# Class attention with swapped context matmuls and spread denominators, and a projection stage with two sets of accumulators

## What is computed

```python
# token attention
scores = einsum('bqhd,bkhd->bhqk', q, k) / sqrt(d)
ctx = einsum('bhqk,bkhd->bqhd', softmax(scores), v)
y = ctx @ Wo.T + bo + emb
h = (y - y.mean((1, 2))) / sqrt(y.var((1, 2)) + 1e-5)     # over a whole sequence
# recurrent attention, its inputs, from x = layernorm(h) over the last axis
q, k = l2norm(x @ Wq), l2norm(x @ Wk)                     # per head
v = x @ Wv;  beta = sigmoid(x @ Wbeta);  gate = silu(x @ Wg)
```

## Time and profile before

| | us |
|---|---|
| median of three executions | 996.98 |
| profiled execution, its own time | 998.3 |
| its span in the profile | 996.3 |
| attention block, from 31.2 to 132.4 | 101.2 |
| statistics block, to 142.6 | 10.2 |
| projection block, to 268.1 | 125.5 |
| PE, DVE, ACT, POOL busy over the span | 761.4, 669.1, 309.6, 424.3 |

### The profile page before, as it was taken

One profiled execution on the slowest core, in us unless ns is written; L12 is line 12 of the kernel. 1 busy time (PEld: TensorE's weight loads), 2 busy tenths in 40 slices (PEclk: granted clock), 3 DMA queues, 4 the chain that ended last, 5 costly groups with the idle time before them and its releaser, 6 DMA issues. The chain is left out here.

```text
span 996.3 us, 20604 instructions
## 1 busy us (share of the span) xinstructions
PE 761.4 (76%) x7708; PEld 521.3 (52%) x7708; DVE 669.1 (67%) x1047; ACT 309.6 (31%) x488; POOL 424.3 (43%) x225
## 2 busy tenths in 40 slices
PE   3589856677588888888888888885777659968653
PEld 3478733333366666666666666664555433322221
DVE  2697756767789999999999999992556530100104
ACT  2433403323233333333333333332444421110100
POOL 1543100000069999999999999982111100000000
PEclk9686978888899999999999999995999978976875
DMA  4000010000000100000000000002911059999946
GB/s 98 1 0 0 0 43 0 0 0 0 13 7 12 34 13 11 11 11 11 11 11 11 11 11 11 12 12 66 359 32 44 1 192 386 410 414 420 409 172 211
DMA packets 48889, 86.31 MB, mean 87 GB/s; under 512 B 5232, under 2 KB 32432, under 8 KB 48848
## 3 DMA queue, kind: packets, MB, share of 16 engines
q1 hardware_dynamic: 43248, 81.23, 22.1%
q10 hardware_dynamic: 5600, 4.53, 1.4%
HBM read 76.31 MB, written 9.44 MB: 86 GB/s over the span
## 5 line engine op out<-in xcount | busy, mean ns | idle before, releaser
L809 POOL TENSOR_TENSOR read<-state,q_pos 128x1024 f32<-128x1024 f32 x128 | 301.7, 2361 | 43.6 <-DVE state L904 34.5
L904 DVE TENSOR_TENSOR_SCAN state<-fac,ps_up 128x1024 f32<-128x1024 f32 x128 | 291.7, 2282 | 12.3 <-ACT fac L853 8.4
L853 ACT ACTIVATE fac<-ps_xf 128x1016 f32<-128x1016 f32 x128 | 130.3, 1018 | 232.1 <-PE ps_xf L934 232.1
L934 PE MATMUL ps_up<-hot,utab 64*128 64x128 f32 x2048 | 148.4, 284 | 38.0 <-DVE state L904 35.6
L934 PEld LDWEIGHTS ps_up<-hot,utab 64*128 64x128 f32 x2048 | 126.6, 189 | 88.6 <-DVE state L904 49.5
L934 PE MATMUL ps_xf<-hot,xtab 64*128 64x128 f32 x2048 | 139.1, 275 | 0.0
L818 POOL TENSOR_TENSOR utab<-tab 128x1024 f32 (+1 forms) x32 | 64.5, 2015 | 160.0 <-SPq L85 160.0
L934 PEld LDWEIGHTS ps_xf<-hot,xtab 64*128 64x128 f32 x2048 | 127.1, 189 | 0.8
L975 PE MATMUL ps_o<-read,sel 128*32 128x256 f32 x1024 | 81.8, 392 | 4.2 <-POOL read L809 4.2
L895 DVE TENSOR_TENSOR xtab<-tab,ps_k 128x1024 f32<-128x1024 f32 x64 | 76.6, 1197 | 1.5 <-PE ps_k L926 1.5
L373 POOL TENSOR_TENSOR logit<-score,logc 128x1024 f32<-128x1024 f32 x16 | 39.4, 2470 | 63.5 <-ACT prob L433 38.1
(11 more groups left out here) (206 smaller groups left out, 969.7 us busy)
## 6 DMA issues: line engine op xcount, KB each, us to landing
w_sb<-in_L_ffn_w SPq DMA_DIRECT2D x32, 2048.0 KB, 19.4
rec_out<-osb SPq DMA_DIRECT2D x128, 32.0 KB, 1.5
ao<-rec_out SPq DMA_DIRECT2D x8, 512.0 KB, 4.0
out_dram<-res ACTq DMA_DIRECT2D x8, 512.0 KB, 2.8
tok<-in_x SPq DMA_DIRECT2D x2, 512.0 KB, 8.3
exp_out<-eo SPq DMA_DIRECT2D x8, 128.0 KB
oq<-exp_out SPq DMA_DIRECT2D x2, 512.0 KB, 3.7
w_nat<-in_L_tok_Wq SPq DMA_DIRECT2D x1, 256.0 KB, 9.7
```

Of the source, the lines that this page charges most:

```text
L809: nc.gpsimd.tensor_tensor(read[n % 2][:], state[n % 4][:].rearrange("p (b i t) -> p b i t", b=2, i=IB), q_pos[x.s][:, :, x.k].unsqueeze(2) ...
L853: nc.scalar.activation(fac[n % 2][:].rearrange("p (n t) -> p n t", t=T)[:, :, 1:], ps_x[:].rearrange("p (n t) -> p n t", t=T)[:, :, 1:], A ...
L904: nc.vector.tensor_tensor_scan(state[n % 4][:], fac[n % 2][:], ps_u[n % 2][:], 0.0, ALU.mult, ALU.add)\
L934: last = nc.tensor.matmul(dst[:, b * 512 + col * T:b * 512 + (col + 1) * T], stationary[rows], pos[rows], start=True, stop=True)
```

## The change

In attention:

- The context matmuls swap operands. The stationary operand is now `v_pair` of a head pair (32 columns), the moving one the transposed probability (128 columns), and the result lands in the 32 PSUM partitions of column group `q = g % 4`. The context comes out transposed, so the transposes (L488) and the copies (L444) go. A second set of eight matmuls with `ones_pair` gives the denominators, each repeated over the 16 rows of its head: 32 instructions a pair instead of 16, and a denominator tile of 256 columns.
- The reciprocal is therefore taken over 128x256 elements instead of 128x16.
- The maxima go to PSUM (`ps_top`), so that the subtraction has one input in SBUF and one in PSUM.
- `ps_t` exists once instead of twice. The copy of the row into `h_tab` moves from DVE to ACT (`keep_row`).
- All engines step by pair: DVE does softmax of a pair, `output` of the pair two before, `finish` of the pair before. The last softmax is followed by two half turns instead of two turns.

In the inputs of the recurrence:

- Statistics and loop are one block. The row's own inverse root is taken from the same call of `inverse_root` as the sequence's (32 elements), so one call and four operations go.
- `x1` is formed straight from the raw row; the normalised row in `h_tab` is written by ACT in the loop (`hidden_rows`).
- `ps_qk`, `ps_vg` and the beta accumulator exist twice. PE waits separately for the copy of q, k and for v, gate; ACT squares first and copies q, k straight into `tab`.
- The norms of both pairs of a turn are found in one pass (64 elements), and rows are normalised two turns ahead.
- The activation table is loaded once, before the loop.

```diff
-            nc.vector.tensor_tensor(v_pair[:, :, 0:2 * D].rearrange("p g (s d) -> p g s d", d=D),
-                                    v_tab[:].rearrange("p (g s d) -> p g s d", s=2, d=D),
+            nc.vector.tensor_tensor(v_pair[:], v_tab[:].rearrange("p (g s d) -> p g s d", s=2, d=D),
                                     half.unsqueeze(3).broadcast_to([P, HP, 2, D]), ALU.mult)
-            ch.link(nc.vector.tensor_copy(v_pair[:, :, 2 * D:], half.broadcast_to([P, HP, 2])))
+            ch.link(nc.vector.tensor_copy(ones_pair[:], row_half[:].unsqueeze(2).broadcast_to([P, 2, D])))
...
-        ps_t = [ctx.enter_context(nc.psum_tensor(f"ps_t{i}", [P, HP * P], F32)) for i in range(2)]
-        ps_c = [ctx.enter_context(nc.psum_tensor(f"ps_c{i}", [P, 512], F32)) for i in range(2)]
+        ps_t = ctx.enter_context(nc.psum_tensor("ps_t", [P, HP * P], F32))
+        ps_c = [ctx.enter_context(nc.psum_tensor(f"ps_c{i}", [P, 2, KT, P], F32)) for i in range(2)]
+        ps_top = ctx.enter_context(nc.psum_tensor("ps_top", [P, 512], F32))
...
+            with eng.Fori(1, TURNS) as t:
+                if enter:
+                    enter(t)
+                for s in range(2):
+                    work(t, s, True, True, True)
+            return [(TURNS, s, False, s == 0, True) for s in range(2)]
...
+                top = ps_top[:, s * H:(s + 1) * H]
                 dve.wait_ge(sc_ok[s], START + i + 1)
-                ch.link(nc.vector.reduce_max(top[s][:], logit[s][:], AX.X))
-                nc.vector.tensor_tensor(logit[s][:], logit[s][:], top[s][:].unsqueeze(2).broadcast_to([P, H, C]),
+                ch.link(nc.vector.reduce_max(top, logit[s][:], AX.X))
+                nc.vector.tensor_tensor(logit[s][:], logit[s][:], top.unsqueeze(2).broadcast_to([P, H, C]),
                                         ALU.subtract).then_inc(lg_ok[s], 1)
 
             def finish(i, s):
                 dve.wait_ge(cx_mm[s], START + i + 1)
-                c = ps_c[s][:, 0:HP * (2 * D + 2)].rearrange("p (g n) -> p g n", g=HP)
-                ch.link(nc.vector.reciprocal(rden[s][:], c[:, :, 2 * D:]))
-                nc.vector.tensor_tensor(cx[s][:].rearrange("p (g s d) -> p g s d", s=2, d=D),
-                                        c[:, :, 0:2 * D].rearrange("p g (s d) -> p g s d", d=D),
-                                        rden[s][:].unsqueeze(3).broadcast_to([P, HP, 2, D]),
-                                        ALU.mult).then_inc(cx_ok[s], 1)
-
-            def output(i, s, r):
+                ch.link(nc.vector.reciprocal(rden[s][:], ps_c[s][:, 1].rearrange("p k c -> p (k c)")))
+                nc.vector.tensor_tensor(cx_t[s][:].rearrange("p k c -> p (k c)"),
+                                        ps_c[s][:, 0].rearrange("p k c -> p (k c)"), rden[s][:], ALU.mult)\
+                    .then_inc(cx_ok[s], 1)
...
                 dve.wait_ge(y_mm[s], START + i + 1)
-                ch.link(nc.vector.tensor_tensor(yrow[s][:], ps_y[s][:, E:2 * E], base[:], ALU.add))
+                dve.wait_ge(h_ok[s], START + i)
+                nc.vector.tensor_tensor(yrow[s][:], ps_y[s][:, 0:E], base[:], ALU.add).then_inc(y_ok[s], 1)
+                dve.wait_ge(y_ok[s], START + i + 1)
                 ch.link(nc.vector.bn_stats(bn[s][:], yrow[s][:]))
-                nc.vector.tensor_copy(stats6[:, bass.ds(r, 1)], bn[s][:].unsqueeze(1))
-                nc.vector.tensor_copy(h_tab[:, bass.ds(r, 1)], yrow[s][:].unsqueeze(1)).then_inc(y_ok[s], 1)
+                nc.vector.tensor_copy(stats6[:, bass.ds(2 * i + s, 1)], bn[s][:].unsqueeze(1))
+            def work(t, s, new, old, older):
                 if new:
-                    softmax_input(t, 0)
+                    softmax_input(t, s)
                 if older:
-                    for s in range(2):
-                        finish(t - 2, s)
-                if new:
-                    softmax_input(t, 1)
-                if older:
-                    for s in range(2):
-                        output(t - 2, s, 2 * (t - 2) + s)
-
-            step(0, older=False)
-            step(1, older=False)
-            with nc.vector.Fori(2, TURNS) as t:
-                ch.enter(t, 2 * 4, 2)
-                step(t)
+                    output(t - 1, s)
+                if old:
+                    finish(t - 1 + s, 1 - s)
...
+            def keep_row(i, s):
+                act.wait_ge(y_ok[s], START + i + 1)
+                nc.scalar.copy(h_tab[:, bass.ds(2 * i + s, 1)], yrow[s][:].unsqueeze(1)).then_inc(h_ok[s], 1)
+
+            def work(t, s, new, old, older):
                 if old:
-                    copy_prob(t - 1, 0)
+                    copy_prob(t - 1 + s, 1 - s)
                 if new:
-                    exponential(t, 0)
-                if old:
-                    copy_prob(t - 1, 1)
+                    exponential(t, s)
                 if older:
-                    for s in range(2):
-                        copy_context(t - 2, s)
...
         def _(pe):
             def transpose_prob(i, s):
                 pe.wait_ge(ex_ok[s], START + i + 1)
-                pe.wait_ge(pt_ok[s], START + i)
                 for g in range(HP):
-                    last = nc.tensor.transpose(ps_t[s][:, g * P:(g + 1) * P], prob[s][:, g * P:(g + 1) * P], ident[:])
+                    last = nc.tensor.transpose(ps_t[:, g * P:(g + 1) * P], prob[s][:, g * P:(g + 1) * P], ident[:])
                 last.then_inc(pt_mm[s], 1)
 
             def context(i, s):
                 pe.wait_ge(pt_ok[s], START + i + 1)
                 pe.wait_ge(cx_ok[s], START + i)
-                n = 2 * D + 2
-                for g in range(HP):
-                    last = nc.tensor.matmul(ps_c[s][:, g * n:(g + 1) * n], prob_t[s][:, g], v_pair[:, g],
-                                            start=True, stop=True)
+                for n in range(2):
+                    for g in range(HP):
+                        k, q = divmod(g, HP // KT)
+                        stationary = (ones_pair[:] if n else v_pair[:, g]).rearrange("p s d -> p (s d)")
+                        last = nc.tensor.matmul(ps_c[s][32 * q:32 * q + 32, n, k], stationary, prob_t[s][:, g],
+                                                start=True, stop=True)
...
+            def work(t, s, new, old, older):
+                if older:
+                    project(t - 1, s)
                 if old:
-                    for s in range(2):
-                        transpose_context(t - 1, s)
-                    for s in range(2):
-                        project(t - 1, s)
-
-            step(0, old=False)
-            with nc.tensor.Fori(1, TURNS) as t:
-                step(t)
-            step(TURNS, new=False)
+                    context(t - 1 + s, 1 - s)
+                if new:
+                    transpose_prob(t, s)
...
-            ch.link(nc.vector.tensor_scalar(varb[:], ps[:, 1, 0:PAIRS], EPS, None, ALU.add))
-            inverse_root(nc, ch, varb[:], rstd_b[:], ex2[:])
-
-            ch.link(nc.vector.tensor_tensor(mean_1[:], dm[:], rstd_b[:], ALU.mult))
-            ch.link(nc.vector.tensor_tensor(var1[:], var_r, rstd_b[:], ALU.mult))
-            ch.link(nc.vector.tensor_tensor(var1[:], var1[:], rstd_b[:], ALU.mult))
-            ch.link(nc.vector.tensor_scalar(var1[:], var1[:], EPS, None, ALU.add))
-            inverse_root(nc, ch, var1[:], rstd_1[:], ex2[:])
+            ch.link(nc.vector.tensor_scalar(varb[:, 0], ps[1][:, 0:PAIRS], EPS, None, ALU.add))
+
+            ch.link(nc.vector.scalar_tensor_tensor(varb[:, 1], varb[:, 0], EPS, var_r, ALU.mult, ALU.add))
+            flat = [v[:].rearrange("p n r -> p (n r)") for v in (varb, rstd)]
+            inverse_root(nc, ch, flat[0], flat[1], newton[:, 0:2 * PAIRS])
+            nc.vector.scalar_tensor_tensor(shift_b[:], mean_b[:], -1.0, rstd[:, 0], ALU.mult, ALU.mult)\
+                .then_inc(sh_ok, 1)
...
+                r = 2 * i + s
+                dve.wait_ge(xt_mm[s], START + i)
+                nc.vector.tensor_scalar(x1[s][:].unsqueeze(1), h_tab[:, bass.ds(r, 1)], mean_row[:, bass.ds(r, 1)],
+                                        rstd[:, 1, bass.ds(r, 1)], ALU.subtract, ALU.mult).then_inc(x_ok[s], 1)
...
+            def norms(i):
+
+                for s in range(2):
+                    dve.wait_ge(raw_ok[s], START + i + 1)
+                both = [v[:].rearrange("p s h -> p (s h)") for v in (norm2, rnorm)]
+                nc.vector.reduce_sum(both[0], sq[:].rearrange("p s h d -> p (s h) d"), AX.X).then_inc(rd_ok, 1)
+                dve.wait_ge(rd_ok, START + i + 1)
+                ch.link(nc.vector.tensor_scalar(both[0], both[0], 1e-24, None, ALU.max))
+                inverse_root(nc, ch, both[0], both[1], newton[:])
...
+                for s in range(2):
+                    values(i, s)
+                    if ahead:
+                        rows(i + 2, s)
+                norms(i)
+                for s in range(2):
+                    table(i, s)
...
```

(36 more changed lines are left out.)

256 lines of the change are left out of this document (101 added, 155 removed).

## The result

The changed kernel takes 963.38 us (median of 4 runs, 960.83 to 964.76), the kernel before 996.75 us in the runs beside it (4 runs, 993.08 to 998.99): a ratio of 0.966, 95% interval 0.963 to 0.969. The profiled execution took 960.83 us, 2.1 of it outside its span.

A forecast was written before the change was run, and what follows sets the result against it. Orders of waits were taken to bound both stages, with DVE working without a gap in attention. From 998.3 us, attention gives -1 and statistics with loop -31.8, making 965.5 us; range 950 to 981.

The forecast's parts named there:

- Reciprocal: Attention, on DVE: growing from 16 to 256 elements, it takes 1.64 us at 5.8 ns for each further element.
- Rivals A: Attention: the reciprocal is cheap (0.5 us), the PE chain bounds, 947 us in all; chance 0.08.
- B: Attention: the reciprocal's slope is steeper, 8.2 ns an element, 2.2 us for 256, 975 us in all; chance 0.10.
- Half turn of attention: Attention: DVE's softmax, `output` and `finish` sum to 5.58 us against 5.47 before, DVE still the bound.
- Subtraction: Attention: the other pair's subtraction loses its extra 1.08 us because one input moves to PSUM, as L895 shows.
- Rival D: Attention: the change does not remove the subtraction's port wait, PSUM operand or not; 974 to 983 us; chance 0.05.
- Rival C: Attention: small copy L413 meets POOL's L373 if `output` is 0.3 us late; in all half turns 995 us; chance 0.03.
- Statistics: Before the projection loop: fewer root operations and one barrier less save 3.9 us, first row for PE at 139.2.
- The weight loads: Statistics stage: issued at the start, they land in that time as before, so they cost nothing.
- What bounded the loop before: Projection loop, 15.25 us a turn: PE waits for single accumulators to be emptied, ACT pays a 1.28 us table load.
- The ring: Changed projection loop: the cycle of waits through ACT and DVE sets a turn of 11.1 us with semaphores.
- Rival E: Whole kernel slower: TensorE stays at 1.2 GHz and PE bounds the loop, 1013 us; chance 0.03.

The follow-up runs named there:

- recip_copy: Changed kernel with a copy of the same 256 denominators in place of their reciprocal (context scaled wrongly): 942.12 us.
- ctx_twice: Changed kernel with every context product of a pair issued twice, 64 matmuls instead of 32, same result: 965.46 us.
- Top_sbuf: Changed kernel with the maxima back in SBUF, in a tile of their own, instead of PSUM: 961.16 us.
- single_acc: Changed kernel with single instead of doubled accumulators for q, k and for v, g: 993.66 us.
- before_preload: Kernel before the change, with the Sigmoid table requested once ahead of its projection loop: 995.03 us.
- wait_hidden: Changed kernel with ScalarE's wait for tables moved from before the square to before the sigmoids, and both pairs' rows written after both activations: 952.19 us.

## Why the prediction was right, and where it was not

The time was forecast at 965.5 us and is 963.4; attention at -1 us (-0.3 in the profile; some +1 over the kernels of the table that leave its work alone), statistics and loop at -31.8 (-35.5). The total meets better than its terms, in part by luck: the forecast starts from the profiled execution, 998.3 us, 1.5 above the median; the two profiled executions differ by 37.5 us and the medians by 33.4, where 32.8 were forecast. So the terms count, not the 2 us. By the steps:

- **Reciprocal**: 1.64 us forecast from a slope of 5.8 ns, 1.75 measured at 6.25 ns. The two rows of other sizes gave the size of an instruction 16 times longer to 7%. Rivals A (0.5 us) and B (2.2 us) fall. VectorE: DVE Perf Modes of the Trainium skill (section "Walkthrough: the 8-slice pipeline in each mode") gives the division a repeat count of 8 and no time per element. The prediction's estimate of 2.13 us plus start-up takes that as 8 cycles an element, and is above what is measured: 6.25 ns are 6.0 cycles of the 0.96 GHz used there.
- **Half turn of attention**: 5.58 forecast, 5.65 measured; the excess is the reciprocal's. That VectorE stays the bound: shown (recip_copy, ctx_twice).
- **Subtraction "loses its extra 1.08 us because one input moves to PSUM"**: the size was right, the cause wrong. Top_sbuf has it without PSUM. The argument from L895 was sound about the hardware and did not ask whether the collision still occurs in the new order, which the same sum (addition from 3.75 us on, next subtraction at 5.6 + 1.2) would have told. Rival D, which priced PSUM as failing at 8 to 17 us, could for this reason not have come.
- **Rival C**, the small copy beside GpSimd: all 16 took 171 ns. The copy starts at 57.08, GpSimd at 57.39: the 0.3 us of the forecast, and no `output` was late enough to use them up.
- **Statistics**: 6.5 us forecast from first operation to first row, 136.55 - 130.13 = 6.4 measured (the forecast's own terms give 4.0 less, not 3.9). The weight loads, "I cost them at nothing": wrong, they became the wait.

```profile
138.21 1.12 PE L680 MATMUL ps_x<-ident,x 128*128 128x128 f32 x4 [4.68 <-DMA w_all<-in_L_attn_Wbeta]
```

  The row for TensorE is there at 136.55 + 0.41 = 136.96; its transposes wait until 138.21, 1.25 us longer, for the last weights. Two things meet. The statistics are shorter, 6.4 us instead of the 10.4 that covered the loads before. And the loads do not start "as before". The last of them, in the kernel before, then in the changed one:

```profile
134.78 0.47 SPq L553 DMA_DIRECT2D w_all<-in_L_attn_Wbeta  x1
```

```profile
133.96 0.47 SPq L548 DMA_DIRECT2D w_all<-in_L_attn_Wbeta  x1
```

  That is 2.1 us behind the first statistics operation (132.71) before, and 3.8 behind it (130.13) now; from issue to landing it takes 4.2 us in both. All eleven kernels here with the new stage issue the first load 1.9 us behind that operation, the three with the old one 0.1. Issued as before, the last weights would by these numbers (an estimate) have landed 6.3 us behind it, before the row was there at 6.8. Why the loads start later stays open. From the first row to the first values 10.25 us pass (136.55 to 146.80) where 7.4 stood (139.2 to 146.6); 1.25 is the weights, most of the rest the first projection, which takes 6.65 us (139.49 to 146.14), longer at the lower clock than in the kernel before, where it took 5.1 (144.91 to 150.00).
- **What bounded the loop before**: "PE waiting for ACT and DVE to empty the single accumulators" is borne out: in the old loop TensorE sat idle ahead of `ps_qk` for 6.5 us until VectorE's L629 and 5.7 us until ScalarE's L680, and in the new one single accumulators cost 29 us (single_acc). "ACT paying a table load of 1.28 us in each turn" is the step that failed. The load was seen on the engine and not asked whose work it delays (before_preload). The sum escaped the error because the new turn was built from its own ring, not by subtracting from the old one.
- **The ring**: 11.1 us forecast, 10.45 measured: the mis-sized term. ScalarE's part to the second pair's values is 1.61 + 2.07 = 3.7 us (168.11 to 169.72 to 171.79 in the same timeline) where 1.7 + 2.4 stood: the second pair's square starts 0.50 us after the rows begin, and operations of ScalarE overlap by up to 0.1 us each. VectorE's part is 178.56 - 171.79 = 6.77 against 6.85, and the 0.15 us added for semaphores did not come on top. From the second pair's first values to its last it is 72.0 us (150.90 to 222.91) where seven turns of 11.1 made 77.7: 5.7 less, of which the slower start of the loop takes back 2.6 and the end gives 0.6. That is the 3.7 us between 31.8 and 35.5.
- **"`hidden_rows` is on the ring, and if ACT were faster, DVE would be the bound at 9.4"**: wait_hidden shows VectorE as the bound, at 9.02, once the rows and the wait for the tables have moved; the share of the rows alone was not measured.
- **Rival E**, the lower clock: the loop had 0.88, and 1.00 in its middle turns. TensorE's pauses are shorter with two accumulators; with one, and the longer pauses, single_acc has 0.82. (The chances named for "faster" add up to 0.94 even without the half-effects, not to 0.93.)

Both errors of cause have one form: a long instruction was seen, and what it cost was taken from its length, not from what waited for its end.

## What to carry to other kernels

When a loop alternates between engines through one accumulator, doubling it can be worth more than thinning the work around it: here 29 of 35 us hung on it, and a quarter less work for VectorE, with the rest of the change, brought 6 without it. What a stall is worth changes with the order around it: the same table request was worth under 2 us in one loop and 14 in the next, so price it by who waits for its end. And when a division moves to a layout that needs it 16 times as often, cost those elements first: here a tidy layout for TensorE, which had room, was paid for by the engine that had none, and the old layout in the new order is 19 us faster. It is the division that costs, not the swap of the operands: with the division left out the swapped form has the shortest attention stage of all, 78.2 us. When a stage gets shorter, ask also of each transfer that it covered when it is issued.
